# Cross attention and spectral layer on one core: the second and third key-row fill put at the end of their slot, and the context normalised ahead of the zero test with its low half first

## What is computed

```
y = layernorm(x)
q, k, v = y @ wq + bq, ctx @ wk + bk, ctx @ wv + bv      (16 heads of 32)
score = (q k^T / sqrt(32)) * mask;  score = where(score == 0, -1e9, score)
x = x + (softmax(score) v) @ wo + bo
x = x + real(ifft(fft(layernorm(x)) @ w)) + bias
```

## Time and profile before

| | |
|---|---|
| median of three runs | 460.57 us (460.48 to 462.78) |
| the profiled execution's own time | 462.53 us |
| its span, first to last instruction | 460.7 us |
| PE busy | 443.5 us (96%) |
| DVE busy | 399.7 us (87%) |
| ACT busy | 373.1 us (81%) |
| POOL busy | 362.7 us (79%) |
| mean granted TensorE clock | 0.996 |
| chain that ended last | PE 77%, DVE 10%, issue 4%, DMA 3% |

### The profile page before, as it was taken

The page is one execution under the profiler, slowest core; times in us unless marked ns, Lnnn a source line. Parts: engine busy times, 40 slices in busy tenths (PEclk is TensorE's granted clock), DMA queues, the critical chain, the costliest instruction groups (busy, mean ns, idle before and its releaser), DMA issues.

```text
span 460.7 us, 11172 instructions
## 1 busy us (share of the span) xinstructions
PE 443.5 (96%) x3510; PEld 293.2 (64%) x3510; DVE 399.7 (87%) x630; ACT 373.1 (81%) x1434; POOL 362.7 (79%) x540
## 2 busy tenths in 40 slices
PE   7989898998999999999999999999999999999997
PEld 5777676675666666666666666666666666555444
DVE  3797599899999999999999999999999898999443
ACT  3358587889898989899989898999989888999620
POOL 6588754795889899797989897979899686976663
PEclk9999999998999999999999999999999999999999
DMA  8997653322435454545545545355433334331244
GB/s 286 393 366 183 231 190 72 106 74 72 95 83 140 125 142 117 140 121 133 125 133 110 144 108 149 84 144 125 120 90 73 92 74 98 70 93 23 70 106 123
DMA packets 85287, 60.16 MB, mean 131 GB/s; under 512 B 40141, under 2 KB 72813, under 8 KB 84718
## 3 DMA queue, kind: packets, MB, share of 16 engines
q1 hardware_dynamic: 84508, 59.29, 47.4%
q10 hardware_dynamic: 722, 0.17, 0.2%
HBM read 29.33 MB, written 8.39 MB: 82 GB/s over the span
## 4 chain that ended last, share of the span: by engine, by line
PE 77%; DVE 10%; issue 4%; DMA 3%; SPq 2%; ACT 2%; POOL 1%; DVEq 0%; POOLq 0%; ACTq 0%
PE bank L438 33%; PE bank L525 17%; PE bank L582 10%; PE bank L599 7%; PE scores L570 5%; DVE zs L860 3%; PE bank L595 3%; PE bank L443 2%; SPq L276 2%; DMA cxs<-in_ctx 2%; DMA xs<-in_x 1%; DVE zs L867 1%; DVE nmin L872 1%; DVE st L897 1%; PE scores L443 1%
## 5 line engine op out<-in xcount | busy, mean ns | idle before, releaser
L688 ACT ACTIVATE zs<-zs,nbias 128x128 f32<-128x128 f32 x512 | 199.6, 397 | 5.2 <-POOL nbias L1093 5.2
L688 ACT ACTIVATION_READ_ACCUMULATOR zs<-zs,nbias 128x1 f32 x512 | 99.5, 194 | 0.0
L867 DVE SCALAR_TENSOR_TENSOR zs<-zs 128x1024 f32<-128x1024 f32 x64 | 80.7, 1262 | 2.3
L860 DVE TENSOR_TENSOR zs<-scores,ms 128x1024 f32<-128x1024 f32 x64 | 78.0, 1218 | 0.3 <-issue 0.3
L872 DVE TENSOR_REDUCE nmin<-zs 128x8 f32<-128x1024 f32 x64 | 77.4, 1209 | 0.1
L525 PE MATMUL bank<-xth,wqh 128*128 128x256 f16 x256 | 70.9, 277 | 2.9 <-DVE kl L810 2.0
L697 ACT COPY pt<-bank 128x512 f32<-128x512 f32 x128 | 68.5, 587 | 5.7 <-PE bank L582 5.2
L525 PE MATMUL bank<-xth,wql 128*128 128x256 f16 x256 | 70.2, 274 | 0.0
L525 PE MATMUL bank<-xtl,wqh 128*128 128x256 f16 x256 | 70.2, 274 | 0.0
L582 PE MATMUL bank<-ident,zs 128*128 128x128 f32 x512 | 67.0, 274 | 0.5 <-ACT zs L688 0.4
L1053 POOL TENSOR_TENSOR xs<-xs,bob 128x512 f32<-128x512 f32 (+1 forms) x41 | 42.3, 1035 | 24.6 <-DVE zs L867 24.6
(11 more groups left out here) (118 smaller groups left out, 965.3 us busy)
## 6 DMA issues: line engine op xcount, KB each, us to landing
xs<-in_x SPq DMA_DIRECT2D x16, 512.0 KB, 4.1
xtr<-in_xt SPq DMA_DIRECT2D x16, 512.0 KB, 4.5
out<-x SPq DMA_DIRECT2D x31, 256.0 KB, 2.5
qs<-qh SPq DMA_DIRECT2D x120, 64.0 KB
lp<-in_lparts SPq DMA_DIRECT2D x4, 1024.0 KB, 9.7
qs<-ql SPq DMA_DIRECT2D x60, 64.0 KB
ms<-in_mask SPq DMA_DIRECT2D x16, 128.0 KB, 2.3
wqs<-in_wq SPq DMA_DIRECT2D x2, 512.0 KB, 6.5
```

The lines of the kernel that those rows point to most:

```text
L688: last = act.activation(z, z, ACT.Exp, bias=nbias[:, s % 4, i:i + 1], scale=-NEG, accum_out=zsum[:, s % 4, i:i + 1])
L860: dve.tensor_tensor(zs[:, s % NZ], A[:].rearrange("p t (h k) -> p t h k", h=4), ms[:, c % NM].unsqueeze(2).broadcast_to([128, 2, 4, KEYS]) ...
L867: dve.scalar_tensor_tensor(out=z, in0=z, scalar=0.0, in1=z, op0=ALU.is_equal, op1=ALU.subtract).then_inc(eq_done, 1)
```

## The change

Three edits. In `plan()`, Z0 and Z1 leave the middle fills of slot 3 and become the first late fills of that slot: TensorE makes them behind the scores of step 4 and the PV of step 0, and ACT and DVE take them in slot 4 as held fills. Their numbers, and those of all other fills, stay. In DVE's slots `ctx_norm` goes ahead of `zero_to_neg`. In POOL's slots `ctx_lo` goes from behind `norm_lo2` and the additions to right behind `bias`. In ACT's slot 3 `split_hi` now stands behind the middle fills.

```diff
     early = {
-        2: [("V", 0), ("ST", 2)], 3: [("V", 1), ("Y", 0), ("Z", 0), ("Z", 1)],
+        2: [("V", 0), ("ST", 2)], 3: [("V", 1), ("Y", 0)],
...
         late = [("Q",) + f for f in queries.get(v, [divmod(v + 9, 4)]) if f[0] < NC]
+        if v == 3:
+            late = [("Z", 0), ("Z", 1)] + late
...
                 for n in held:
                     hi(n)
+                for n in mids:
+                    hi(n)
                 if v == 3:
                     split_hi(3)
-                for n in mids:
-                    hi(n)
...
                     mask_mul(v)
+                if 0 <= v - 4 < NS:
+                    ctx_norm(v - 4)
                 if 0 <= v < NS:
                     zero_to_neg(v)
-                if 0 <= v - 4 < NS:
-                    ctx_norm(v - 4)
...
                     bias(v)
+                if 0 <= v - 4 < NS:
+                    ctx_lo(v - 4)
...
                 if v == 3:
                     low_o()
-                if 0 <= v - 4 < NS:
-                    ctx_lo(v - 4)
```

## The result

The changed kernel takes 462.63 us (median of 20 runs, 462.00 to 464.19) against 460.94 us for the kernel before in the same measurement (20 runs, 460.33 to 462.78): ratio 1.0037, 95% interval 1.0029 to 1.0046. That is 1.7 us slower, a real difference, but under the 0.5% that I had called the line.

The account below looks back on a forecast made before the run. It took TensorE to bound the kernel from 120 to about 390 us, and DVE, started by chunk 4's x load, between 60 and 80. Sum: 460.57 + 3.9 - 1.4 = 463.1 us, range 462.2 to 465.0.

Parts of the forecast that it names:

- Part 1: Z0 and Z1 moved to the end of slot 3: costs 2.2 + 1.7 = 3.9 us, between 2.2 and 4.6.
- The clock was to cost 1.7: TensorE's granted clock falls behind the new gap ahead of U0, costing 1.7 us, bounds 0 and 2.4.
- the clock doesn't fall: Rival: the clock stays up behind the new gap ahead of U0, giving 461.4 us; chance 0.12.
- not slower: Rival: DVE has slack in slots 3 and 4 and the filled wait ahead of Z0 counts, 457.9 us; chance 0.10.
- The upper end of 4.6: Cost of moving Z0 and Z1 if the low clock lasts through PV and the transposes of slot 5: 4.6 us.
- SP at nothing: SP's row copies and loads start later, but its queue is free 1.4 us before `stack_q` of chunk 2: no cost.
- Part 2: `ctx_norm` ahead of the zero test on DVE: gains 1.5 us where the low stretch occurs, otherwise nothing.
- the low stretch: Low TensorE clock at 112 us, in the profiled execution, perhaps not in median ones; would explain most of 1.96 us.
- DVE is busy throughout there, so little of the 1.0 of the wait alone is kept: Around 111 us, removing TensorE's 1.02 us wait for `cn` by itself gains little, as DVE is busy.
- Part 3: `ctx_lo` behind `bias` on POOL: two waits for `cl` near the end go, 1.4 us gained, between 0 and 1.4.
- a sign against part 3: If waits for `cl` remain in the changed profile, the claim for `ctx_lo` behind `bias` is wrong.
- POOL and DVE get in each other's way: Rival: POOL's longer operation starts ahead of the zero test, DVE waits up to 0.9 us, 464.0 us; chance 0.11.

Follow-up runs that it names:

- keep_busy: The changed kernel with 26 idle products put on TensorE ahead of U0: 462.08 us, ratio 1.0011.
- z_only: The kernel before with only the move of the Z0 and Z1 fills: 465.99 us, ratio 1.0095.
- cn_only: The kernel before with only `ctx_norm` put ahead of the zero test on DVE: 460.05 us, ratio 0.9967.
- cn_cl: The changed kernel without its move of Z0 and Z1, so `ctx_norm` and `ctx_lo` moved only: 458.58 us, ratio 0.9930.
- null: The kernel before, unchanged, run again for a second trace: 461.59 us, ratio 1.0003.
- cl_only: The kernel before with only `ctx_lo` put right behind `bias` on POOL: 460.57 us, ratio 0.9973.
- z_taken_in_slot: The changed kernel, but ACT and DVE take Z0 and Z1 in slot 3 while TensorE still makes them late: 458.61 us, ratio 0.9930.
- cn_cl_x4_pool: cn_cl with GpSimd's spread ahead of `norm_lo2` from slot 54 and chunk 4's x loaded ahead of tables and last weight part: 459.56 us, ratio 0.9972.
- fixed_x4: The changed kernel with Z0 and Z1 taken within slot 3 and chunk 4's x loaded ahead of tables and last weight part: 458.53 us, ratio 0.9954.

## Why the prediction was right, and where it wasn't

The forecast was 463.1 us and the measurement 462.63. The sum is right to half a microsecond, but one of its terms was missed, and a base that was too low made up for part of it.

**Part 1, forecast +3.9: right, in size and in mechanism.** U0 was to start 4.59 us behind the start of DVE's slot 4 (62.6 - 58.01) and started 4.71 behind it. DVE was to lose 2.6 us up to slot 5; with the clock kept up it loses (68.71 - 58.17) - (65.69 - 58.01) = 2.9. Of it 2.2 were to reach the PV of slot 6; at full clock it is (79.57 - 57.63) - (75.99 - 58.01) - 1.44 = 2.5. The clock was to cost 1.7 and cost 1.44 in the traced execution. Together 3.96. Against the kernel with edits 2 and 3 alone, the changed kernel loses 3.6 us in the profiled executions (462.08 - 458.50), 4.05 by the medians and 4.9 by the ratios; edit 1 alone loses 4.4. The spread has a source on record: against 458.58 the 11 executions with a mean clock of 0.996 lose 3.6 and the 9 with 0.993 lose 4.8. The rival "the clock doesn't fall" is out by the windows, and "not slower", which had DVE's mask product of slot 5 at 65.7, by its 69.62.

The upper end of 4.6, which the Trainium skill's rule on transposes (TensorE: Matmul & The Clock Gate, Part 4) would have given, is not what the trace shows: the granted clock was 1.00 again from 68 us on, and the eight transposes at 69.58 took 1.04 us, as those at full clock at 56.86 did. The rule itself isn't tested by this: the clock was up before they began.

**SP at nothing: right for the queue.** The row copies ran from 62.92, and the queue was free at 70.0, well ahead of the stacking of the queries at 74.06. But I had looked only at the queue. The stacking itself, 14 DMAs from the freed Q to the scores of step 8, moved by the same 4 us as the rest of the chain; these scores wait 0.26 us for it in the changed kernel. In keep_busy they wait 1.35, but there the train from its first DMA to the scores took 13.3 us instead of 12.2; with 12.2 the wait would be about 0.25 (an estimate from these rows). So a second chain stood right behind the one I costed, and moved with it.

**Part 2, forecast 0 on the median and -1.5 with the low stretch: wrong.** Between steps 4 and 8 the traces that have the edit take 26.3 to 26.9 us and the others 28.6 to 29.0, among them two without the low stretch; some 2 us of it stay where the later start of step 4 is taken off. In the time it is 0.5 to 1.3 us against executions of before at full clock for edit 2 alone, which then waits 1.68 us for `cl`, and 2.0 beside edit 3 (460.57 to 458.58), where I had put nothing. The step that failed is "DVE is busy throughout there, so little of the 1.0 of the wait alone is kept". A busy DVE keeps nothing of a wait only if its own work stays the same; here the zero test left the path of `cn`, and one of DVE's operations took 0.69 us instead of 1.71 because it no longer met GpSimd's. I had read rows 9 as a risk of the change. The same collision stood in the kernel before at 105 us, and the change took it away there. My account of the low stretch was right in that it isn't in every execution and costs 1.5. That the wait for `cn` brings it on isn't shown: z_only has that wait and not the stretch.

**Part 3, forecast -1.4: the mechanism right, the size wrong.** The two waits of 0.62 and 0.79 us shrink to 0.23, so waits for `cl` remain, which I had named as a sign against part 3, and a wait of 0.57 us for `cl` is new at 117 us. In the tail this brings 0.4 alone and 0.56 with edit 2, since waits of 0.82 and 0.44 us for `rzb` come in their place. This is the rival "POOL and DVE get in each other's way", which I priced at 0.9 us: the zero test that met `norm_lo2` took 2.13 us instead of 1.22, 0.9 more, as rated (0.6 more than the 1.50 of the earlier trace rows); only that its price is paid out of the 1.4, not on top of the forecast. The Trainium skill, SBUF: State Buffer, section Who interferes with whom, says that an operation of DVE with two SBUF inputs and one of GpSimd that reads SBUF lock each other out, the first to start winning. The traces agree in both directions: at 105 us DVE starts first and GpSimd's operation takes 1.63 us (cn_only), and at 403 us GpSimd starts first and the zero test, whose two inputs are the same tile, takes 2.13. What edit 3 brings besides, I had not seen: between steps 8 and 12 it keeps `cl` from becoming the next wait behind edit 2 (25.33 against 26.45).

So edits 2 and 3 bring 2.85 us where I had 1.4, and the median of before, with more runs, lies 0.1 to 0.9 above the 460.57 on which I built (0.37 in the measurement of the result). With the numbers of the set of cn_cl the sum is 461.43 - 2.85 + 4.05 = 462.63; mine was 460.57 - 1.4 + 3.9 = 463.07. The gain that I missed, 1.45 us, is offset by a base 0.86 too low and a part 1 that costs 0.15 more: the errors nearly cancel, and the closeness of the sum is in part luck. The median of 462.63 itself depends on how many of the 20 executions are of the kind with a mean clock of 0.993.

## What to carry to other kernels

Before a fill is moved to "later in the slot", ask when its result is taken: making it later was free here, taking it a slot later cost 4 us, because the next user of the bank waited behind it. Look in the timeline of the old kernel for single instructions that take longer than their like (1.71 against 0.68 us); a reordering that looks neutral may remove or create such a collision, and that can be worth more than the waits it was made for. A wait that TensorE shows names the last link only: shortening that link (the spread, 1.4 to 0.4 us) brought nothing while the next thing that TensorE needed, the exponentials, came no sooner.

## What the runs showed of the hardware

Whether TensorE's clock falls can differ between executions of one program: at 112 us the kernel before lost about 1.5 us in 14 of 36, and with edit 3, which changes little there, the mean clock was 1.000 in 11 of 11. The wait just before doesn't decide it alone in these traces: behind a wait of 1.02 us the level fell in before and null and not in z_only and cl_only, and behind a wait of 1.59 or 1.60 us at 69 us it fell in z_taken_in_slot and cn_cl_x4_pool (0.50 from 71 us on) and not in cn_cl. Sets without the low stretch also scatter less: 0.3 to 0.4 us from fastest to slowest with edit 2 (459.92 to 460.23; 458.45 to 458.86) and 0.2 for the 12 executions of before in the set of fixed_x4, against 2.4 us and more for the sets of before that have it. And a GpSimd copy that takes 0.40 us alone takes 1.39 when DVE's zero test, which reads SBUF twice, has started ahead of it (404.07 beside 403.09).
